# Rotary layer attention of an adaLN block: keys and queries normalised in place in PSUM, negated scores, another order of the norms

## Chip, core and metric

One core of a Trainium2 chip runs the whole block in one launch. The metric is device microseconds of that core, from the first to the last instruction of an execution. Engines are called as in the profile: PE (TensorE, PEld are its weight loads), DVE (VectorE), ACT (ScalarE), POOL (GpSimd), SP (SyncE).

## What is computed

The block takes 4 x 1024 tokens of width 256. A modulated layer norm is followed by a causal attention with 16 heads, then a second modulated norm is followed by two "layers", whose result is gated and added. The change touches only the local attention of those two layers (8 heads of 64, QK_SCALE 8, windows of 128 tokens that see themselves and the window before):

```python
def _layer(x, wqkv, qs, ksc, wo, lg, lb, w1, b1, w2, b2):
    h = shift_token(x)                       # second half of the channels from the token before
    q, k, v = split(h @ wqkv, 3)
    q = l2norm(q) * qs                       # per head of 64
    k = l2norm(k) * ksc
    q = q*cos*scale + rotate_half(q)*sin*scale
    k = k*cos/scale + rotate_half(k)*sin/scale
    sim = 8 * q k^T                          # own window and the one before
    sim = where(mask, -max, sim)
    x = x + (softmax(sim) @ v) @ wo
    ...                                      # shift, norm, gated gelu MLP, added to x
```

## The kernel before, in words

The work falls into phases: the first norm, the causal attention (about 1240 us), `phase_layers` (the rest but the last 30 us) and the output. `phase_layers` runs a loop over two layers. In each, the attention loops over 32 tiles of 128 tokens, two tiles to a turn of the hardware loop (`par` 0 and 1), and then an MLP loops over 8 chunks. Each engine has its instruction stream written out by hand, and semaphores order them. An engine takes its instructions strictly in the order written, so what stands behind a waiting instruction waits too.

The tiles are software-pipelined. In one turn for tile t:

- PE transposes probabilities of tile t (`probs_T`, L1407), multiplies them with the values (`values`, L1417), makes the scores (`scores`, L1397) of tile t and then t+1, projects tile t+2 (`project`, parts 2 for v, 0 for q, 1 for k; the lines are those of the helper, L74 to L76), transposes the rotated q and k of tile t+1 (`qk_T`, L1389), transposes the stream of tile t+3 (`stream_T`, L1367), the output (`out_T`, L1424) and projects it (`project_out`, L74 to L76).
- DVE rotates q and k of tile t+1 (`rotate`, L1171 and L1174), masks the scores and takes their maxima (`maxima`, L1203), makes the exponent's bias from maximum and inverse norm (L1206), the low halves of the split operands (L1195, L1152, L1153, L1221), the sums of squares of tile t+2 (`squared_norms`, L1160 and L1162) and the normalised output (`normalise_out`, L1212 and L1216), and adds to the stream (L1321).
- ACT takes the exponentials (`exps`, L1018), copies transposed probabilities out of PSUM (`copy_probs`, L1027), the high halves of q and k (`qk_hi`, L1006 and L1008), the squares (`squares`, L1001) and the high half of the output (`out_hi`, L1031).
- POOL raises the sums of squares to the power -0.5 (`inverse_norms`, L928 and L929), adds the two rotated parts (`add_rotated`, L933), stages a tile (L920) and carries one column from tile to tile (`carry_over`, L915 and L917).

The query's norm is not applied to q: it enters as the `scale` of the exponential, and in its bias. The key's norm is applied by one multiplication out of PSUM into the tile `ly_kn` in SBUF (L1186), from which the key is rotated.

The orders that matter below, of ACT and of DVE in the second half of a turn, and of PE there:

```python
# ACT
exps(l, t, g, 3, par); qk_hi(l, t + 1, 1 - par, 0); copy_probs(g, 3); qk_hi(l, t + 1, 1 - par, 1)
squares(l, t + 2, 0); squares(l, t + 2, 1); stream_hi(l, t + 3, 1 - par); out_hi(g)
# DVE
maxima(l, t, g, 3, par); qk_lo(..., 0); qk_lo(..., 1); normalise_out(g, par); stream_lo(l, t + 3, 1 - par)
maxima(l, t + 1, g + 1, 0, ...); out_lo(g); squared_norms(l, t + 2, 0); maxima(l, t + 1, g + 1, 1, ...)
squared_norms(l, t + 2, 1); x += ...
# PE
qk_T(l, t + 1, 0); qk_T(l, t + 1, 1); values(g, 2, v_slots); probs_T(g, 3); project(l, t + 2, par, 1)
values(g, 3, v_slots); stream_T(...); scores(l, t + 1, 0, ...); out_T(g); scores(l, t + 1, 1, ...); project_out(g)
```

Of the kernel before, what the change touches and what calls it, by code (L numbers as in the profile page):

```python
# [725 lines left out]
def phase_layers(nc, io, scr, keep):  # L726
# [5 lines left out]
    with ExitStack() as ctx:  # L732
# [18 lines left out]
        rq = a.sb("ly_rq", [P, 2, LH])  # L751
        rk = a.sb("ly_rk", [P, LH])
        kn = a.sb("ly_kn", [P, INNER])
# [5 lines left out]
        small = a.sb("ly_small", [P, 2, 2, 2])  # L759
# [6 lines left out]
        def cut(start, *shape):  # L766
# [3 lines left out]
            if len(shape) > 1:  # L770
# [41 lines left out]
                 "mx_done nb_done h_lo rc_done on_done red_done fl_done ra_done kn_done o_lo qkT_lo xa_done msk "  # L812
# [5 lines left out]
        DVE_SEMS = ("mx_done nb_done h_lo rc_done on_done red_done fl_done ra_done kn_done o_lo qkT_lo xa_done msk "  # L818
# [36 lines left out]
        with nc.Block() as block:  # L855
# [37 lines left out]
            def _(pool):  # L893
# [28 lines left out]
                def inverse_norms(l, t, par, extra=0):  # L922

                    n = nth_rotated(l, t)

                    hold(pool, s["tick"], (s["fl_done"], at(2 * nth_projected(l, t) + 2)), (s["kn_done"], at(n)),
                         (s["ex_done"], at(LP * (nth(l, t) - 1) + extra)))
                    pool.tensor_tensor(rk[:], norm2[:, 1, 1, :], expo[:], ALU.pow).then_inc(s["pw_done"], 1)  # L928
                    pool.tensor_tensor(rq[:, par, :], norm2[:, 0, 1, :], expo[:], ALU.pow).then_inc(s["pw_done"], 1)  # L929
# [10 lines left out]
                with pool.Fori(0, L) as l:  # L940
                    hold(pool, s["tick"], (s["ya_done"], at(NCH * l)))
                    stage_tile(0, 0)
                    stage_tile(1, 1)
                    carry_over(l, 0, 0, 0)
                    stage_tile(0, 2)
                    inverse_norms(l, 0, 0, LP)
                    add_rotated(l, 0, 0)
                    add_rotated(l, 0, 1)
                    carry_over(l, 1, 1, 1)
                    stage_tile(1, 3)  # L950
                    inverse_norms(l, 1, 1)
                    carry_over(l, 2, 0, 2)
                    with pool.Fori(0, B) as b, pool.Fori(0, TB // 2) as jj:
                        for par in range(2):
                            t = b * TB + jj * 2 + par
                            add_rotated(l, t + 1, 0)
                            add_rotated(l, t + 1, 1)
                            hold(pool, s["tick"], (s["xT_mm"], at(nth_transposed(l, t + 3))))
                            stage_tile(par, (t + 4) % NT)
                            carry_over(l, t + 3, 1 - par, (jj * 2 + par + 3) % TB)  # L960
                            inverse_norms(l, t + 2, par)
                    inverse_deviation(l, 0)
                    with pool.Fori(0, NCH) as c:
                        hold(pool, s["tick"], (s["xnd"], at(nth_norm(l, c) + 1)))
                        pool.tensor_tensor(x[:, ds(c * CT, CT), :], x[:, ds(c * CT, CT), :],
                                           b2[:].unsqueeze(1).broadcast_to([P, CT, D]), ALU.add).then_inc(s["b2_done"], 1)
                        inverse_deviation(l, c + 1)

            @block.scalar
            def _(act):  # L970
# [44 lines left out]
                def exps(l, t, g, j, par):  # L1015
                    hold(act, s["tick"], (s["nb_done"], at(nth_scores(l, t, j) + 1)))
                    for h in range(2):
                        step = act.activation(pr[:, j % 2, h, :], sm[:, j % 2, h, :], ACT.Exp,  # L1018
                                              bias=small[:, j % 2, 1, h:h + 1], scale=rq[:, par, 2 * j + h:2 * j + h + 1],
                                              accum_out=sums[:, par, 2 * j + h:2 * j + h + 1])  # L1020
                    step.then_inc(s["ex_done"], 1)
# [91 lines left out]
            def _(dve):  # L1113
# [63 lines left out]
                def rotate_q(l, t, w):  # L1177
                    rotate(l, t, 0, ps_qkv[0][:], w)

                def rotate_k(l, t, w):  # L1180
                    after(dve, "kn_done", nth_rotated(l, t) + 1)
                    rotate(l, t, 1, kn[:], w)

                def normalise_keys(l, t):
                    after(dve, "pw_done", 2 * nth_projected(l, t) + 1)
                    dve.tensor_tensor(kn[:].rearrange("p (h d) -> p h d", d=DH), ps_qkv[1][:].rearrange("p (h d) -> p h d", d=DH),  # L1186
                                      rk[:].unsqueeze(2).broadcast_to([P, LH, DH]), ALU.mult).then_inc(s["kn_done"], 1)
# [9 lines left out]
                def maxima(l, t, g, j, par):  # L1197

                    if j >= 2:
                        after(dve, "ex_done", LP * g + j - 1)  # L1200
                    hold(dve, s["tick"], (s["sc_mm"], at(nth_scores(l, t, j) + 1)))
                    for h in range(2):
                        dve.tensor_tensor_reduce(sm[:, j % 2, h, :], ps_s[h][:, 0:2 * P], mask[:, par].rearrange("p a b -> p (a b)"),  # L1203
                                                 1.0, -3.0e38, ALU.add, ALU.max, small[:, j % 2, 0, h:h + 1]).then_inc(s["mx_done"], 1)
                    after(dve, "mx_done", 2 * nth_scores(l, t, j) + 2)
                    dve.scalar_tensor_tensor(small[:, j % 2, 1, :], small[:, j % 2, 0, :], -1.0, rq[:, par, 2 * j:2 * j + 2],  # L1206
                                             ALU.mult, ALU.mult).then_inc(s["nb_done"], 1)
# [61 lines left out]
                with dve.Fori(0, L) as l:  # L1269
# [10 lines left out]
                    rotate_q(l, 0, 0)  # L1280
                    normalise_keys(l, 0)
                    rotate_k(l, 0, 0)
# [12 lines left out]
                    with dve.Fori(0, B) as b, dve.Fori(0, TB // 2) as jj:  # L1295
                        for par in range(2):
# [3 lines left out]
                            rotate_q(l, t + 1, w)  # L1300
                            maxima(l, t, g, 2, par)
                            normalise_keys(l, t + 1)
                            rotate_k(l, t + 1, w)
# [8 lines left out]
                            qk_lo(l, t + 1, 1 - par, 1)  # L1312
                            normalise_out(g, par)
# [3 lines left out]
                            squared_norms(l, t + 2, 0)  # L1317
                            maxima(l, t + 1, g + 1, 1, 1 - par)
                            squared_norms(l, t + 2, 1)
# [39 lines left out]
            def _(pe):  # L1359
# [10 lines left out]
                def project(l, t, par, i):  # L1370
# [6 lines left out]
                    if i == 1:  # L1377
                        after(pe, "kn_done", n)
# [82 lines left out]
                with pe.Fori(0, L) as l:  # L1461
# [17 lines left out]
                    with pe.Fori(0, B) as b, pe.Fori(0, TB // 2) as jj:  # L1479
                        for par in range(2):  # L1480
# [16 lines left out]
                            qk_T(l, t + 1, 1)  # L1497
                            values(g, 2, v_slots)
                            probs_T(g, 3)
                            project(l, t + 2, par, 1)  # L1500
# [10 lines left out]
                         (s["nb_done"], at((LP * NT + 2) * (l + 1))), (s["xa_done"], at(NT * (l + 1))))  # L1511
# [33 lines left out]
def rope_tables():  # L1545
# [11 lines left out]
    tables = np.stack([cos * scale, sin * scale, cos / scale, sin / scale]).astype(np.float32)  # L1557
# [3 lines left out]
def local_masks():  # L1561

    q, k = np.arange(P)[:, None], np.arange(P)[None, :]
    own = np.where(k <= q, 0.0, MASKED).astype(np.float32)
    before = np.where(k >= q, 0.0, MASKED).astype(np.float32)
    none = np.full((P, P), MASKED, np.float32)
# [56 lines left out]
```

## Time and profile before

| | before |
|---|---|
| device time, median of 3 runs | 2997.27 us |
| the three runs | 2996.97, 2997.27, 2999.57 us |
| profiled execution, first to last instruction | 2999.0 us |
| busy PE / DVE / ACT / POOL | 2509.8 / 2103.4 / 1630.0 / 864.7 us |
| PE, weight loads | 1960.9 us |
| mean granted TensorE clock, whole span | 0.949 |
| attention loops of the two layers, from their first tile | about 1303 to 1856 us and 2162 to 2713 us |

The page gives for the profiled execution its span; no longer time is listed for it, and the span lies within the range of the three runs. Busy time is a sum over phases with different limits. The two attention loops of the layers take about 1100 us of the span, and what a turn of them costs has to be read from its own timeline.

### The profile page before, as it was taken

The page shows a single profiled execution, that of the slowest core. Times are in us where ns is not written, and L with a number is a line of the kernel's source. Part 1 is how long each engine was busy: PE and PEld are TensorE (multiplying, and loading weights), DVE is VectorE, ACT ScalarE, POOL GpSimd, SP SyncE. Part 2 cuts the span into 40 slices and gives each one's busy share as a digit, 9 for nine tenths or more (in the row PEclk, how much of TensorE's full clock was granted, in tenths as well). Part 3 has the DMA queues.
Part 4 walks back from the last instruction along what each step waited for, and adds up shares of the span by engine and source line. Part 5 has one row for each costly group of instructions (what it writes and reads, how often), then busy time and mean ns, then how long its engine had stood idle before and what let it go on. Part 6 is the DMA issues. An engine that isn't in the chain of part 4 may idle for free. (4 is left out here: it accounts for less than half of the span.)

```text
span 2999.0 us, 68027 instructions
## 1 busy us (share of the span) xinstructions
PE 2509.8 (84%) x22296; PEld 1960.9 (65%) x22296; DVE 2103.4 (70%) x4501; ACT 1630.0 (54%) x3100; POOL 864.7 (29%) x732
## 2 busy tenths in 40 slices
PE   5699989989998998188998895799698989894996
PEld 3466656666666666177777774688577777773885
DVE  5588668858885885667777775566577777774656
ACT  2566556646664674356666664333466666662332
POOL 0233223313331332333333332111233333332111
PEclk7899999999999999599999998899899999997998
DMA  4400020010002000400000000100100000000003
GB/s 154 143 11 16 5 73 11 13 65 14 13 10 68 11 15 19 140 1 0 7 1 6 4 3 6 45 0 0 34 0 7 0 7 0 7 0 7 0 0 112
DMA packets 74546, 77.26 MB, mean 26 GB/s; under 512 B 4224, under 2 KB 67320, under 8 KB 72952
## 3 DMA queue, kind: packets, MB, share of 16 engines
q1 hardware_dynamic: 74488, 76.46, 7.8%
q8 instruction: 40, 0.66, 0.1%
q14 instruction: 18, 0.15, 0.0%
HBM read 55.48 MB, written 16.78 MB: 24 GB/s over the span
## 5 line engine op out<-in xcount | busy, mean ns | idle before, releaser
L501 ACT ACTIVATE at_p<-at_ps_s,at_shift 128x1024 f32<-128x1024 f32 (+3 forms) x384 | 343.0, 902 | 112.1 <-DVE at_p_lo L435 50.3
L74 PE MATMUL ly_ps<-ly_w_hi,ly_operands 128*128 128x256 f32 (+1 forms) x1048 | 372.6, 356 | 33.6 <-DVE ly_operands L1221 17.2
L435 DVE TENSOR_TENSOR at_p_lo<-at_p,at_p_hi 128x1024 f16<-128x1024 f32 (+3 forms) x384 | 391.4, 1019 | 12.1
L1018 ACT ACTIVATE ly_probs<-ly_masked,ly_small,ly_rq 128x256 f32<-128x256 f32 x512 | 303.5, 594 | 145.2 <-DVE ly_small L1206 145.0
L431 DVE CAST at_p_hi<-at_p 128x1024 f16<-128x1024 f32 (+3 forms) x384 | 283.0, 737 | 140.9 <-PE at_ps_o L569 100.9
L75 PE MATMUL ly_ps<-ly_w_lo,ly_operands 128*128 128x256 f32 (+1 forms) x1048 | 347.4, 332 | 0.0
L76 PE MATMUL ly_ps<-ly_w_hi,ly_operands 128*128 128x256 f32 (+1 forms) x1048 | 346.5, 331 | 0.0
L567 PE MATMUL at_ps_o<-at_v,at_p_hi 128*128 128x65 f16 x2304 | 249.5, 194 | 36.0 <-DVE at_p_lo L435 36.0
L567 PEld LDWEIGHTS at_ps_o<-at_v,at_p_hi 128*128 128x128 f16 x2304 | 209.6, 96 | 99.9 <-DVE at_p_lo L435 56.1
L1417 PEld LDWEIGHTS ly_ps<-ly_values,ly_probs_T 128*128 128x128 f32 x2048 | 258.5, 191 | 12.3 <-issue 0.8
L1417 PE MATMUL ly_ps<-ly_values,ly_probs_T 128*128 x2048 | 256.7, 268 | 0.0
L74 PEld LDWEIGHTS ly_ps<-ly_w_hi,ly_operands 128*128 128x128 f32 x1048 | 202.1, 193 | 73.3 <-issue 31.6
L568 PE MATMUL at_ps_o<-at_v,at_p_hi 128*128 128x64 f16 x2304 | 247.7, 194 | 0.0
L569 PE MATMUL at_ps_o<-at_v,at_p_lo 128*128 128x65 f16 x2304 | 246.1, 192 | 0.0
L74 PE MATMUL at_ps_m<-at_hT,at_w_hi 128*128 (+1 forms) x396 | 176.3, 445 | 65.0 <-DVE at_v L400 43.6
L1027 ACT ACTIVATE ly_probs_T<-ly_ps 128x512 f32<-128x512 f32 x256 | 150.4, 587 | 139.9 <-PE ly_ps L1417 121.7
L1203 DVE CUSTOM_DVE_ANT_0 ly_masked<-ly_ps,ly_mask 128x256 f32<-128x256 f32 x520 | 198.7, 419 | 24.7 <-DVE ly_mask L1308 11.7
L76 PEld LDWEIGHTS ly_ps<-ly_w_hi,ly_operands 128*128 128x128 f32 x1048 | 202.2, 193 | 19.1
L569 PEld LDWEIGHTS at_ps_o<-at_v,at_p_lo 128*128 128x128 f16 x2304 | 213.7, 99 | 0.0
L568 PEld LDWEIGHTS at_ps_o<-at_v,at_p_hi 128*128 128x128 f16 x2304 | 213.3, 97 | 0.4
L1195 DVE TENSOR_TENSOR ly_operands<-ly_ps,ly_operands 128x512 fp32r<-128x512 f32 x132 | 91.3, 692 | 173.0 <-ACT ly_operands L1006 128.6
L1397 PE MATMUL ly_ps<-ly_operands 64*128 64x256 f32 x1560 | 161.9, 313 | 60.6 <-DVE ly_small L1203 60.6
(208 smaller groups left out, 6331.1 us busy)
## 6 DMA issues: line engine op xcount, KB each, us to landing
at_hT<-hT_hi SPq DMA_DIRECT2D x5, 1024.0 KB, 5.0
at_hT<-hT_lo SPq DMA_DIRECT2D x5, 1024.0 KB, 8.1
at_w_raw<-in_Wv SPq DMA_DIRECT2D x34, 128.0 KB, 2.1
at_w_raw<-in_Wq SPq DMA_DIRECT2D x34, 128.0 KB, 2.3
at_w_raw<-in_Wk SPq DMA_DIRECT2D x34, 128.0 KB, 2.3
n_x<-in_states SPq DMA_DIRECT2D x4, 1024.0 KB, 11.6
hT_hi<-n_hi SPq DMA_DIRECT2D x8, 512.0 KB, 3.0
hT_lo<-n_lo SPq DMA_DIRECT2D x8, 512.0 KB, 3.1
```

What stands on the lines that cost most here:

```text
L74: pe.matmul(out, w_hi, x_hi, start=first, stop=False, skip_group_check=True)
L75: pe.matmul(out, w_hi, x_lo, start=False, stop=False, skip_group_check=True)
L76: return pe.matmul(out, w_lo, x_hi, start=False, stop=last, skip_group_check=True)
L431: dve.tensor_copy(p_hi[u % 2][:, :, off:], probs[u % 2][:, :, off:]).then_inc(p_hi_done, 1)
L435: dve.tensor_tensor(p_lo[u % 2][:, :, off:], probs[u % 2][:, :, off:], p_hi[u % 2][:, :, off:], ALU.subtract).then_inc(p_lo_done, 1)
L501: act.activation(probs[u % 2][:, :, off:], ps_s[u % 2][:, :, off:], ACT.Exp, bias=shift[:], scale=SCORE_SCALE).then_inc(exp_done, 1)
L567: pe.matmul(out, ph, ones_hi, start=(kt == 0 and t == 0), stop=False, skip_group_check=True)
L568: pe.matmul(out[:, 0:DH], ph, lo, start=False, stop=False, skip_group_check=True)
L569: step = pe.matmul(out, pl, ones_hi, start=False, stop=(kt == qc * CT + t), skip_group_check=True)
L1018: step = act.activation(pr[:, j % 2, h, :], sm[:, j % 2, h, :], ACT.Exp, bias=small[:, j % 2, 1, h:h + 1], scale=rq[:, par, 2 * j + h:2 * ...
L1203: dve.tensor_tensor_reduce(sm[:, j % 2, h, :], ps_s[h][:, 0:2 * P], mask[:, par].rearrange("p a b -> p (a b)"), 1.0, -3.0e38, ALU.add, ALU ...
L1417: step = pe.matmul(ps_pv[:, cols], pT[:, (2 * slot + h) * P:(2 * slot + h + 1) * P], vv[:, v_slots[slot], cols], start=(j == 0 and h == 0 ...
```

## The change

- q is no longer left unnormalised. POOL raises the norms of q and then of k into one tile `rn`; DVE multiplies q and k with them in place in PSUM and rotates both from PSUM (`normalise_and_rotate`). The SBUF tile `kn` is gone, and the exponential has the constant scale -1.
- The tables that rotate q are negated, so that the scores come out negated; the masks are positive, and the masked minimum is the bias of the exponential itself. The small DVE operation between maxima and exponential (L1206) and its semaphore are gone.
- DVE runs both `squared_norms` of tile t+2 right behind `qk_lo` and ahead of `normalise_out`.
- PE runs `project(t+2, 1)` ahead of `values(g, 2)` instead of behind `probs_T(g, 3)`, and it waits for all six rotations instead of for `kn`.
- POOL runs `inverse_norms(t+2)` ahead of `carry_over(t+3)`, and q's power waits only for q's sum.

Left out of the diff are the lists of semaphores, the calls ahead of the loop, which follow the same pattern, and PE's wait behind the loop, which takes `mx_done` for `nb_done`.

```diff
@@ -748,15 +748,13 @@
         expo = a.sb("ly_expo", [P, LH])
         sq = a.sb("ly_sq", [P, 2, INNER])
         norm2 = a.sb("ly_norm2", [P, 2, 2, LH])
-        rq = a.sb("ly_rq", [P, 2, LH])
-        rk = a.sb("ly_rk", [P, LH])
-        kn = a.sb("ly_kn", [P, INNER])
+        rn = a.sb("ly_rn", [P, 2, LH])
         xs = a.sb("ly_xs", [P, 2, D])
         ra = a.sb("ly_rope_a", [P, 2, INNER])
         rt = a.sb("ly_rope_t", [P, 2, INNER])
         sm = a.sb("ly_masked", [P, 2, 2, 2 * P])
         pr = a.sb("ly_probs", [P, 2, 2, 2 * P])
-        small = a.sb("ly_small", [P, 2, 2, 2])
+        nmax = a.sb("ly_nmax", [P, 2, 2])
         sums = a.sb("ly_sums", [P, 2, LH])
         rsum = a.sb("ly_rsum", [P, LH])
         vv = a.sb("ly_values", [P, V_RING, INNER])
...
@@ -919,14 +917,11 @@
                 def stage_tile(par, tile):
                     pool.tensor_copy(xs[:, par, :], x[:, tile, :]).then_inc(s["xs_done"], 1)
 
-                def inverse_norms(l, t, par, extra=0):
-
-                    n = nth_rotated(l, t)
-
-                    hold(pool, s["tick"], (s["fl_done"], at(2 * nth_projected(l, t) + 2)), (s["kn_done"], at(n)),
-                         (s["ex_done"], at(LP * (nth(l, t) - 1) + extra)))
-                    pool.tensor_tensor(rk[:], norm2[:, 1, 1, :], expo[:], ALU.pow).then_inc(s["pw_done"], 1)
-                    pool.tensor_tensor(rq[:, par, :], norm2[:, 0, 1, :], expo[:], ALU.pow).then_inc(s["pw_done"], 1)
+                def inverse_norms(l, t):
+
+                    for i, used in enumerate(("qn_done", "kn_done")):
+                        hold(pool, s["tick"], (s["fl_done"], at(2 * nth_projected(l, t) + i + 1)), (s[used], at(nth_rotated(l, t))))
+                        pool.tensor_tensor(rn[:, i, :], norm2[:, i, 1, :], expo[:], ALU.pow).then_inc(s["pw_done"], 1)
 
                 def add_rotated(l, t, i):
                     hold(pool, s["tick"], (s["ra_done"], at(6 * nth_rotated(l, t) + 3 * i + 3)))
...
@@ -957,8 +952,8 @@
                             add_rotated(l, t + 1, 1)
                             hold(pool, s["tick"], (s["xT_mm"], at(nth_transposed(l, t + 3))))
                             stage_tile(par, (t + 4) % NT)
+                            inverse_norms(l, t + 2)
                             carry_over(l, t + 3, 1 - par, (jj * 2 + par + 3) % TB)
-                            inverse_norms(l, t + 2, par)
                     inverse_deviation(l, 0)
                     with pool.Fori(0, NCH) as c:
                         hold(pool, s["tick"], (s["xnd"], at(nth_norm(l, c) + 1)))
...
@@ -1013,10 +1008,10 @@
                     act.activation(vv[:, slot, :], ps_qkv[2][:], ACT.Copy).then_inc(s["v_done"], 1)
 
                 def exps(l, t, g, j, par):
-                    hold(act, s["tick"], (s["nb_done"], at(nth_scores(l, t, j) + 1)))
+                    hold(act, s["tick"], (s["mx_done"], at(2 * nth_scores(l, t, j) + 2)))
                     for h in range(2):
                         step = act.activation(pr[:, j % 2, h, :], sm[:, j % 2, h, :], ACT.Exp,
-                                              bias=small[:, j % 2, 1, h:h + 1], scale=rq[:, par, 2 * j + h:2 * j + h + 1],
+                                              bias=nmax[:, j % 2, h:h + 1], scale=-1.0,
                                               accum_out=sums[:, par, 2 * j + h:2 * j + h + 1])
                     step.then_inc(s["ex_done"], 1)
 
...
@@ -1174,17 +1169,14 @@
                         dve.tensor_tensor(th[:, :, a0:a0 + half], zh[:, :, b0:b0 + half],
                                           sin[:, a0:a0 + half].unsqueeze(1).broadcast_to([P, LH, half]), ALU.mult).then_inc(s["ra_done"], 1)
 
-                def rotate_q(l, t, w):
-                    rotate(l, t, 0, ps_qkv[0][:], w)
-
-                def rotate_k(l, t, w):
-                    after(dve, "kn_done", nth_rotated(l, t) + 1)
-                    rotate(l, t, 1, kn[:], w)
-
-                def normalise_keys(l, t):
-                    after(dve, "pw_done", 2 * nth_projected(l, t) + 1)
-                    dve.tensor_tensor(kn[:].rearrange("p (h d) -> p h d", d=DH), ps_qkv[1][:].rearrange("p (h d) -> p h d", d=DH),
-                                      rk[:].unsqueeze(2).broadcast_to([P, LH, DH]), ALU.mult).then_inc(s["kn_done"], 1)
+                def normalise_and_rotate(l, t, i, w):
+
+                    done = ("qn_done", "kn_done")[i]
+                    after(dve, "pw_done", 2 * nth_projected(l, t) + i + 1)
+                    z = ps_qkv[i][:].rearrange("p (h d) -> p h d", d=DH)
+                    dve.tensor_tensor(z, z, rn[:, i, :].unsqueeze(2).broadcast_to([P, LH, DH]), ALU.mult).then_inc(s[done], 1)
+                    after(dve, done, nth_rotated(l, t) + 1)
+                    rotate(l, t, i, ps_qkv[i][:], w)
 
                 def qk_lo(l, t, par, i):
                     after(dve, "qkT_hi", 2 * nth_rotated(l, t) + i + 1)
...
@@ -1200,11 +1192,9 @@
                         after(dve, "ex_done", LP * g + j - 1)
                     hold(dve, s["tick"], (s["sc_mm"], at(nth_scores(l, t, j) + 1)))
                     for h in range(2):
-                        dve.tensor_tensor_reduce(sm[:, j % 2, h, :], ps_s[h][:, 0:2 * P], mask[:, par].rearrange("p a b -> p (a b)"),
-                                                 1.0, -3.0e38, ALU.add, ALU.max, small[:, j % 2, 0, h:h + 1]).then_inc(s["mx_done"], 1)
-                    after(dve, "mx_done", 2 * nth_scores(l, t, j) + 2)
-                    dve.scalar_tensor_tensor(small[:, j % 2, 1, :], small[:, j % 2, 0, :], -1.0, rq[:, par, 2 * j:2 * j + 2],
-                                             ALU.mult, ALU.mult).then_inc(s["nb_done"], 1)
+                        dve.tensor_tensor_reduce(sm[:, j % 2, h, :], ps_s[h][:, 0:2 * P],
+                                                 mask[:, par].rearrange("p a b -> p (a b)"),
+                                                 1.0, 3.0e38, ALU.add, ALU.min, nmax[:, j % 2, h:h + 1]).then_inc(s["mx_done"], 1)
 
                 def normalise_out(g, par):
                     after(dve, "ex_done", LP * g + LP)
...
@@ -1297,10 +1286,9 @@
                             t = b * TB + jj * 2 + par
                             g = nth(l, t)
                             w = (jj * 2 + par + 1) % TB
-                            rotate_q(l, t + 1, w)
+                            normalise_and_rotate(l, t + 1, 0, w)
                             maxima(l, t, g, 2, par)
-                            normalise_keys(l, t + 1)
-                            rotate_k(l, t + 1, w)
+                            normalise_and_rotate(l, t + 1, 1, w)
                             if par == 1:
 
                                 m = (NT // 2 + 1) * l + b * (TB // 2) + jj + 1
...
@@ -1310,13 +1298,13 @@
                             maxima(l, t, g, 3, par)
                             qk_lo(l, t + 1, 1 - par, 0)
                             qk_lo(l, t + 1, 1 - par, 1)
+                            squared_norms(l, t + 2, 0)
+                            squared_norms(l, t + 2, 1)
                             normalise_out(g, par)
                             stream_lo(l, t + 3, 1 - par)
                             maxima(l, t + 1, g + 1, 0, 1 - par)
                             out_lo(g)
-                            squared_norms(l, t + 2, 0)
                             maxima(l, t + 1, g + 1, 1, 1 - par)
-                            squared_norms(l, t + 2, 1)
                             after(dve, "wo_mm", g + 1)
                             dve.tensor_tensor(x[:, t, :], x[:, t, :], ps_misc[:, 0:D], ALU.add).then_inc(s["xa_done"], 1)
                     split_weights(4 * l + 2, F_COLS, 0)
...
@@ -1375,7 +1363,7 @@
                     if i == 0:
                         after(pe, "ra_done", 6 * n - 3)
                     if i == 1:
-                        after(pe, "kn_done", n)
+                        after(pe, "ra_done", 6 * n)
                     cols = slice(i * INNER, (i + 1) * INNER)
                     for k in range(KT):
                         step = three_products(pe, ps_qkv[i][:], hT[:, par, 0, k, 0:P], hT[:, par, 1, k, 0:P],
...
@@ -1495,9 +1483,9 @@
                             qk_T(l, t + 1, 0)
                             after(pe, "v_done", nth_projected(l, t + 2) + 1)
                             qk_T(l, t + 1, 1)
+                            project(l, t + 2, par, 1)
                             values(g, 2, v_slots)
                             probs_T(g, 3)
-                            project(l, t + 2, par, 1)
                             values(g, 3, v_slots)
                             after(pe, "qkT_lo", 2 * nth_rotated(l, t + 1) + 2)
                             stream_T(l, t + 3, 1 - par)
...
@@ -1554,16 +1542,16 @@
     scale = np.concatenate([scale, scale], axis=-1)
     sign = np.where(np.arange(DH) < DH // 2, -1.0, 1.0).astype(np.float32)
     cos, sin = np.cos(freqs), np.sin(freqs) * sign
-    tables = np.stack([cos * scale, sin * scale, cos / scale, sin / scale]).astype(np.float32)
+    tables = np.stack([-cos * scale, -sin * scale, cos / scale, sin / scale]).astype(np.float32)
     return np.ascontiguousarray(tables.reshape(4, TB, P, DH).transpose(2, 0, 1, 3).reshape(P, -1))
 
 
 def local_masks():
 
     q, k = np.arange(P)[:, None], np.arange(P)[None, :]
-    own = np.where(k <= q, 0.0, MASKED).astype(np.float32)
-    before = np.where(k >= q, 0.0, MASKED).astype(np.float32)
-    none = np.full((P, P), MASKED, np.float32)
+    own = np.where(k <= q, 0.0, -MASKED).astype(np.float32)
+    before = np.where(k >= q, 0.0, -MASKED).astype(np.float32)
+    none = np.full((P, P), -MASKED, np.float32)
 
     mask = np.stack([np.stack([own, before], axis=1), np.stack([before, own], axis=1)], axis=1)
     return {"mask": mask, "prev_mask": np.stack([none] + [before] * (TB // 2 - 1), axis=1)}
...
```

## Rows read from the trace of the kernel before

**Rows 1.** Timeline of ACT, L1031, once a tile: start us, us, engine, line, what.

```profile
1299.23 0.60 ACT L1031 ACTIVATE ly_operands<-ly_ps 128x512 fp32r<-128x512 f32 x1 [0.62 <-PE ly_ps L1424]
...
1844.92 0.60 ACT L1031 ACTIVATE ly_operands<-ly_ps 128x512 fp32r<-128x512 f32 x1 [0.62 <-PE ly_ps L1424]
```

**Rows 2.** Waits of PE, 1303 to 1856 us: in total, times, longest.

```profile
PE ly_ps L1397 <- DVE ly_small L1203: 26.8, 31, 1.1
PE ly_ps L1389 <- POOL ly_rope_a L933: 19.7, 30, 0.9
```

**Rows 3.** Timeline of PE, one tile, 1619 to 1638 us.

```profile
1619.66 0.60 PE L1407 MATMUL ly_ps<-ident,ly_probs 128*128 128x128 f32 x4
...
1626.89 0.60 PE L1389 MATMUL ly_ps<-ident,ly_rope_a 128*128 128x128 f32 x4
1628.01 0.66 PE L1389 MATMUL ly_ps<-ident,ly_rope_a 128*128 128x128 f32 x4 [0.52 <-POOL ly_rope_a L933]
1628.50 1.00 PE L1417 MATMUL ly_ps<-ly_values,ly_probs_T 128*128 x8
1629.43 0.66 PE L1407 MATMUL ly_ps<-ident,ly_probs 128*128 128x128 f32 x4
1629.84 0.48 PE L74 MATMUL ly_ps<-ly_w_hi,ly_operands 128*128 128x512 f32 x1
...
1631.32 1.00 PE L1417 MATMUL ly_ps<-ly_values,ly_probs_T 128*128 x8
...
1637.07 0.60 PE L1407 MATMUL ly_ps<-ident,ly_probs 128*128 128x128 f32 x4
```

**Rows 4.** Timeline of ACT in the same tile.

```profile
1630.12 0.60 ACT L1027 ACTIVATE ly_probs_T<-ly_ps 128x512 f32<-128x512 f32 x1 [0.27 <-PE ly_ps L1407]
1630.62 0.59 ACT L1008 ACTIVATE ly_operands<-ly_ps 128x512 fp32r<-128x512 f32 x1
1631.10 1.18 ACT L1001 ACTIVATE ly_sq<-ly_ps 128x512 f32<-128x512 f32 x2
```

**Rows 5.** Timeline of DVE in the same tile.

```profile
1623.22 0.68 DVE L1186 TENSOR_TENSOR ly_kn<-ly_ps,ly_rk 128x512 f32<-128x512 f32 x1
1624.05 0.69 DVE L1171 TENSOR_TENSOR ly_rope_a<-ly_kn,ly_rope 128x512 f32<-128x512 f32 x1
...
1631.85 0.19 DVE L1212 RECIPROCAL ly_rsum<-ly_sums 128x8 f32<-128x8 f32 x1
1632.42 0.69 DVE L1216 TENSOR_TENSOR ly_on<-ly_ps,ly_rsum 128x512 f32<-128x512 f32 x1 [0.38 <-DVE ly_rsum L1212]
...
1635.35 0.67 DVE L1160 TENSOR_REDUCE ly_norm<-ly_sq 128x8 f32<-128x512 f32 x1
...
1636.32 0.42 DVE L1203 CUSTOM_DVE_ANT_0 ly_masked<-ly_ps,ly_mask 128x256 f32<-128x256 f32 x1
...
1637.30 0.69 DVE L1160 TENSOR_REDUCE ly_norm<-ly_sq 128x8 f32<-128x512 f32 x1
...
1638.15 0.42 DVE L1321 TENSOR_TENSOR stream<-stream,ly_ps 128x256 f32 x1
```

**Rows 6.** Durations by line: min/median/max ns; the second is of the page's part 5.

```profile
L1171 DVE TENSOR_TENSOR ly_rope_a<-ly_kn,ly_rope x66: 691/693/1839, 1262.9 to 2698.8; 128x512 f32<-128x512 f32 x66
...
L933 POOL TENSOR_TENSOR ly_rope_a<-ly_rope_a,ly_rope_t 128x512 f32<-128x512 f32 x132 | 175.8, 1332 | 75.8 <-DVE ly_rope_t L1174 75.8
```

**Rows 7.** Stretches: us, busy PE, PEld, DVE, ACT, POOL, PE clock, DMA share, GB/s.

```profile
1315.11:1318.52 3.41, 2.02 (x19) 1.38 (x18) 2.86 (x10) 1.76 (x6) 0.19 (x1) 1.00 0.02 5
1318.53:1321.94 3.41, 3.41 (x16) 3.16 (x16) 2.73 (x10) 1.83 (x6) 0.51 (x1) 0.50 0.02 5
1632.55:1635.96 3.41, 2.27 (x21) 1.66 (x20) 3.06 (x10) 2.05 (x6) 0.19 (x1) 1.00 0.00 0
```

**Rows 8.** Timeline of ACT, L1031, around the second of these stretches.

```profile
1316.61 0.60 ACT L1031 ACTIVATE ly_operands<-ly_ps 128x512 fp32r<-128x512 f32 x1 [0.62 <-PE ly_ps L1424]
1335.39 0.60 ACT L1031 ACTIVATE ly_operands<-ly_ps 128x512 fp32r<-128x512 f32 x1 [0.63 <-PE ly_ps L1424]
```

More of the change, by code:

```diff
@@ L811, in phase_layers @@
                  "h_hi ex_done sq_done pt_done o_hi qkT_hi v_done "
-                 "mx_done nb_done h_lo rc_done on_done red_done fl_done ra_done kn_done o_lo qkT_lo xa_done msk "
+                 "mx_done h_lo rc_done on_done red_done fl_done ra_done qn_done kn_done o_lo qkT_lo xa_done msk "
                  "ca_in ca_out pw_done add_done xs_done "
@@ L817, in phase_layers @@
         ACT_SEMS = "h_hi ex_done sq_done pt_done o_hi qkT_hi v_done w_hi_done warmed ff_done f_hi gl_done"
-        DVE_SEMS = ("mx_done nb_done h_lo rc_done on_done red_done fl_done ra_done kn_done o_lo qkT_lo xa_done msk "
+        DVE_SEMS = ("mx_done h_lo rc_done on_done red_done fl_done ra_done qn_done kn_done o_lo qkT_lo xa_done msk "
                     "w_lo_done rope_q bn ag vr nr xnd f_lo uf_done u_lo ya_done")
@@ L945, in _ @@
                     stage_tile(0, 2)
-                    inverse_norms(l, 0, 0, LP)
+                    inverse_norms(l, 0)
                     add_rotated(l, 0, 0)
@@ L950, in _ @@
                     stage_tile(1, 3)
-                    inverse_norms(l, 1, 1)
+                    inverse_norms(l, 1)
                     carry_over(l, 2, 0, 2)
@@ L1279, in _ @@
                     squared_norms(l, 0, 1)
-                    rotate_q(l, 0, 0)
-                    normalise_keys(l, 0)
-                    rotate_k(l, 0, 0)
+                    normalise_and_rotate(l, 0, 0, 0)
+                    normalise_and_rotate(l, 0, 1, 0)
                     qk_lo(l, 0, 0, 0)
@@ L1510, in _ @@
                     hold(pe, s["tick"], (s["sq_done"], at(2 * (NT + 2) * (l + 1))),
-                         (s["nb_done"], at((LP * NT + 2) * (l + 1))), (s["xa_done"], at(NT * (l + 1))))
+                         (s["mx_done"], at(2 * (LP * NT + 2) * (l + 1))), (s["xa_done"], at(NT * (l + 1))))
                     chunk_T(l, 0)
```

## The prediction

> **What bounds the kernel now.** I read the stretches of the trace first, to find where the changed code runs: two attention loops of 32 tiles each. ACT's copy of the output stands once in each tile, so its first and last start in one loop give the period: (1844.92 - 1299.23) / 31 = 17.60 us [rows 1]. The reader should see there that 64 tiles are 1126 us, and that a microsecond per tile is 64 us of the kernel.
>
> Then the waits of PE. Over one loop they are 26.8 us on the masked scores and 19.7 us on the rotated keys [rows 2], together 46.5 / 31 = 1.5 us per tile. PE works in the other 16: it is nearly the bound, so whatever is to be won here is small, and what makes PE wait longer is paid in full.
>
> Last the timelines of one tile, from one start of the first probability transposition to the next, 1619.66 to 1637.07, 17.41 us [rows 3]. Read backwards from the next tile: project_out waits for the output's low half, that for ACT's copy, that for out_T, and out_T for the normalised output `ly_on` on DVE (1632.42). This DVE operation waits now for the last `values` on PE (begun 1631.32, lasting 1.00) and not for DVE: the reciprocal before it had long begun (1631.85) [rows 3, 5]. So the loop's chain is: PE up to the last values, DVE `ly_on`, then 1637.07 - 1632.42 = 4.65 us of out_T, copy, low half and project_out, then PE again.
>
> **The change part by part.**
>
> *PE's order.* I count from the start of the tile's first transposition. The first qk_T starts at 7.23 and takes about 0.49 (as from the second, 1628.01, to values, 1628.50); the second starts at 8.35, so it waited 8.35 - 7.72 = 0.63 us for the keys [rows 3]. After the change that wait goes (next part). But project(1), 1631.32 - 1629.84 = 1.48 us, now stands ahead of values(2), 0.93 us (1628.50 to 1629.43). The last probs_T starts at 7.72 + 0.49 + 1.48 + 0.93 = 10.62 instead of 9.77. Project(1) was the cover for ACT's copy of these probabilities: the copy starts 0.69 us after probs_T and lasts 0.60 [rows 3, 4], so without cover the last values starts 1.35 us after probs_T instead of 1.89 (0.06 for the handover). That is 11.97, against 11.66: PE alone loses only 0.3 us here, and idles 0.9 us that it had worked.
>
> *The norms ahead of the output.* This is the expensive edit. On ACT the order is unchanged: copy of the probabilities, high half of the keys, the two squares. The copy waits for the last probs_T, so all of them hang on it: high half of the keys 1.19 us, squares 1.67 us after probs_T, and both squares done at 2.85 [rows 3, 4]. DVE takes the low half of the keys and is ready for the reciprocal 1631.85 - 1629.43 = 2.42 us after probs_T [rows 3, 5]. Now two squared norms stand there. One costs DVE 1636.32 - 1635.35 = 0.97 or 1638.15 - 1637.30 = 0.85 us, to the start of what follows [rows 5]; the mean is 0.91, two are 1.82. The squares come in time for them. The reciprocal then starts at 4.24 after probs_T. From it to `ly_on` there are 0.57 us now, in part the wait for PE; without that the reciprocal's own 0.19 and a handover remain, so from 0.27 to 0.57, and I take the middle, 0.42. `ly_on` starts at 4.66 after probs_T instead of 2.99. Behind it wait, on DVE, the low half of the stream and maxima(0) of the next tile; PE has done its scores by then and waits for `ly_on`.
>
> *Sum per tile with the clock as it is.* 10.62 + 4.66 + 4.65 = 19.93 us, against 17.60: 2.33 us more, bounds 2.2 to 2.5 from the handover.
>
> *Normalising in place, and the rotations.* DVE gains an operation per tile, q times its norm. For a write into PSUM no row exists; the nearest is the same multiplication out of PSUM into SBUF, 0.68 us [rows 5]. Below, it could be somewhat faster than that; above, I take twice, 1.4 us. With the wait for itself it fills 1624.05 - 1623.22 = 0.83 us [rows 5]. It loses the small operations between maxima and exponential, four per tile, and rotates the keys from PSUM: from `ly_kn` the first product took 691 ns at best and 1839 at worst, while POOL added [rows 6]. None of this counts in the sum: DVE has the stream's addition behind it about 0.8 us into PE's next tile, then q 0.83 and its rotation 1.26 (as in this timeline), maxima 0.70 (two of 0.35), k 0.83 + 1.26, that is keys rotated at 5.7. POOL adds them in 1.33 [rows 6] and 0.26 of handover, at 7.3, and PE asks for them at 7.72. So there is 0.4 us of room. If the product in PSUM costs double (twice 0.69 us), 1.4 - 0.4 = 1.0 us per tile comes on top. The removed small operation also brings ACT the exponentials earlier, but the last of these is needed at 10.62 and comes at about 9.3.
>
> *POOL's order.* The two powers start right behind q's sum, while DVE is busy with norms and output; q's is needed in the next tile. The carried column is now written behind two powers, and next read by project(2) of the next tile, over 2 us later. Nothing is added. The first tiles of each layer have a little more and a little less in chain, within 2 us for both layers; I take 0.
>
> *The clock.* From the last probs_T on, PE would be busy 0.66, idle 0.7, busy 1.0, idle 0.2, busy 1.0, idle 1.7, busy 0.65 (out_T), idle 0.5, busy 0.6, idle 0.7. The 3.4 us around the largest gap hold about 1.3 us of work. Now, of two stretches of 3.41 us at the same place in a tile, one with 2.27 us of PE work was followed by full clock, one with 2.02 by a stretch of 3.41 us at 0.50, that is 1.2 for 2.4 GHz [rows 7]. The fall at 1318.5 lengthened its tile to 1335.39 - 1316.61 = 18.78 us, 1.2 us over the mean [rows 1, 8]. I expect a fall in nearly every tile. In the new order part of the slow stretch lies over PE's own waits, where it is cheap (about 0.5 us), part over dense projections (3.41 us at half speed do 1.95 us of such work, 1.5 us lost). I take 1.0 per tile, the middle, 64 us in all, bounds 0 and 1.5.
>
> The Trainium skill ("TensorE: Matmul & The Clock Gate", Part 1 with "HAM oscillation") gives as its abstract rule that gaps without any matmul, of a length that no gap of this loop reaches, bring the slow clock. By this rule there would be no fall here, and the time would be that of the first rival. The trace speaks against it: no gap before the fall at 1318.5 was over 1.1 us, PE's longest wait in the loop [rows 2].
>
> **Sum.** 64 x 2.33 = 149 and 64 x 1.0 = 64, together 213 us, on the profiled execution's 2999 us: 3212 us. That execution's span is 2 us above the median of the runs shown, which is 2997; I give 3210.
>
> **The rivals.**
>
> *The clock holds.* For: PE's longest new gap is 1.7 us. Against: the row with 2.02 us of work. It gives 2997 + 149 = 3146 us.
>
> *The write into PSUM is dear.* At double cost the keys come 1.0 us late in every tile, and the order above still holds: 3210 + 64 = 3274 us. For: no DVE operation of this loop writes PSUM, so nothing excludes it. Against: the reads from PSUM cost no more than from SBUF (0.68 us out of PSUM, 0.69 out of SBUF) [rows 5].
>
> *Faster.* If DVE is what the loop hangs on, its lighter stretch (no `ly_kn` slowed by POOL, no small operations) is passed on, and the norms and projections find room in waits. At best all waits of rows 2 go, 1.5 x 64 = 96 us; with the keys' wait alone, 19.7 / 31 x 64 = 41 us, so 2956 us. It decides if `ly_on` does not start later than 3.0 us after a last probs_T that is itself no later than 9.8. For: the keys' wait is real. Against: two norms in series on DVE directly before `ly_on`.
>
> *No change.* The gain of the keys and of the maxima would have to meet the loss of the norms exactly; I see nothing for it.
>
> **How the numbers follow.** Forecast (falls in most tiles) 0.62; clock holds 0.23; dear write 0.07; faster 0.04; the rest, about nothing, 0.02 and a still longer slow clock 0.02. A difference below 0.2%, 6 us, can't be told from none. So slower 0.93, same 0.03, faster 0.04. The range reaches from the clock that holds with the lower handover, 2997 + 64 x 2.2 = 3138, less a little for terms rounded up, 3125, to falls at 1.4 us each, 2997 + 149 + 90 = 3236, and a part of a dear write: 3260.
>
> **What would show it right or wrong.** The distance of two L1031 starts should be near 20.9 us (19.9 if the clock holds). On PE, out_T (L1424) should wait for `ly_on` by over 1.5 us per tile, the last values for the copy by about 0.8, and qk_T no longer for POOL. On DVE, two L1160 should stand between L1195 and L1212. The clock of the loops should be near 0.9 instead of 0.99. It would be wrong if the reciprocal starts less than 3 us after the last probs_T, if PE waits at qk_T for the keys still, or if the period is below 17.6.

## The result, and the profile after

The changed kernel takes 3258.7 us (median of 4 runs, 3255.4 to 3261.7), against 2998.4 us (2997.0 to 3000.3) of the kernel before on the same chip: a ratio of 1.086, 95% interval 1.085 to 1.088. The forecast was 3210 us, range 3125 to 3260. The direction and the mechanism were right, and the time lies at the upper end of the range: one term, the slow clock, was sized too small, and the longer chain somewhat too large.

The period comes from ACT's copy of the output (now L1026), first and last of the first loop, which answers to [rows 1]:

```profile
1298.68 0.60 ACT L1026 ACTIVATE ly_operands<-ly_ps 128x512 fp32r<-128x512 f32 x1 [2.08 <-PE ly_ps L1412]
...
1970.53 0.60 ACT L1026 ACTIVATE ly_operands<-ly_ps 128x512 fp32r<-128x512 f32 x1 [2.55 <-PE ly_ps L1412]
```

(1970.53 - 1298.68) / 31 = 21.67 us, against 17.60. The second loop has 21.64. 64 x 4.07 = 260 us is the whole difference, so it lies in the two loops of 32 tiles. The waits of PE from 1300 to 1840 us (in total, times, longest) answer to [rows 2]:

```profile
PE ly_ps L1412 <- DVE ly_on L1206: 33.9, 25, 1.4
PE ly_ps L1405 <- ACT ly_probs_T L1022: 19.3, 25, 0.8
PE ly_ps L74 <- DVE ly_operands L1211: 16.8, 25, 0.7
PE ly_ps L1355 <- DVE ly_operands L1187: 6.5, 25, 0.3
```

The waits of before, for the masked scores and for the keys, are gone. In their place PE waits, 25 times in 25 tiles, at out_T for the normalised output, at the last values for the copied probabilities, and at project_out. The next two fences are the timelines of PE and then of DVE in one tile; they answer to [rows 3] and [rows 5].

```profile
1618.71 0.61 PE L1395 MATMUL ly_ps<-ident,ly_probs 128*128 128x128 f32 x4
1620.09 1.10 PE L1405 MATMUL ly_ps<-ly_values,ly_probs_T 128*128 x8 [0.77 <-ACT ly_probs_T L1022]
1621.45 0.44 PE L1355 MATMUL ly_ps<-ident,ly_xs 128*128 128x128 f32 x2 [0.26 <-DVE ly_operands L1187]
1621.82 0.63 PE L1385 MATMUL ly_ps<-ly_operands 64*128 64x256 f32 x6
1623.85 1.11 PE L1412 MATMUL ly_ps<-ident,ly_on 128*128 128x128 f32 x4 [1.41 <-DVE ly_on L1206]
...
1626.63 0.55 PE L74 MATMUL ly_ps<-ly_w_hi,ly_operands 128*128 128x256 f32 x1 [0.69 <-DVE ly_operands L1211]
...
1629.33 0.71 PE L1395 MATMUL ly_ps<-ident,ly_probs 128*128 128x128 f32 x4
```

```profile
1621.08 0.68 DVE L1155 TENSOR_REDUCE ly_norm<-ly_sq 128x8 f32<-128x512 f32 x1
...
1621.96 0.69 DVE L1155 TENSOR_REDUCE ly_norm<-ly_sq 128x8 f32<-128x512 f32 x1
...
1622.87 0.20 DVE L1202 RECIPROCAL ly_rsum<-ly_sums 128x8 f32<-128x8 f32 x1
1623.10 0.69 DVE L1206 TENSOR_TENSOR ly_on<-ly_ps,ly_rsum 128x512 f32<-128x512 f32 x1
```

The reader should see the series: the two sums (1621.08, 1621.96), then the reciprocal 4.16 us after the last probs_T (1618.71), `ly_on` 4.39 us after it (before: 2.99), and only then out_T. A second thing shows in the durations: out_T takes 1.11 us. In the kernel before it was

```profile
1633.17 0.66 PE L1424 MATMUL ly_ps<-ident,ly_on 128*128 128x128 f32 x4
```

The clock is low there. Two stretches of the same tile (us, busy PE, PEld, DVE, ACT, POOL, then PE clock), which answer to [rows 7]:

```profile
1615.60:1622.40 6.80, 5.76 (x44) 4.79 (x43) 2.59 (x5) 4.35 (x12) 0.17 (x1) 1.00 0.00 0
1622.80:1629.40 6.60, 4.86 (x23) 4.23 (x24) 3.40 (x14) 2.79 (x9) 2.94 (x4) 0.50 0.00 0
```

For 6.6 us and a little more the clock stands at 0.50, 1.2 GHz. Before it fell, PE had waited 0.77 and 0.26 us, and it was waiting for `ly_on`. It is back at full only with the next tile's first transpositions. In this loop the clock fell once in each of the 31 tiles; 10 of these stretches lasted about 10 us, the others about 6.8.

### The profile page after: what moved, and what is told of

It reads as the page before. It is cut to its first block and busy times, and to the rows that moved or that the text cites. A ratio compares the mean times of both kernels' runs of the same rounds, so it can differ in the third digit from the quotient of the medians.

```text
span 3257.1 us, 67705 instructions
## 1 busy us (share of the span) xinstructions
PE 2684.5 (82%) x22296; PEld 2103.9 (65%) x22296; DVE 2024.0 (62%) x4307; ACT 1569.9 (48%) x3100; POOL 851.0 (26%) x732
## 5 line engine op out<-in xcount | busy, mean ns | idle before, releaser
L74 PE MATMUL ly_ps<-ly_w_hi,ly_operands 128*128 128x256 f32 (+1 forms) x1048 | 415.0, 396 | 60.3 <-DVE ly_operands L1211 43.7
L75 PE MATMUL ly_ps<-ly_w_lo,ly_operands 128*128 128x256 f32 (+1 forms) x1048 | 384.0, 366 | 0.0
L76 PE MATMUL ly_ps<-ly_w_hi,ly_operands 128*128 128x256 f32 (+1 forms) x1048 | 380.0, 363 | 0.0
L924 POOL TENSOR_TENSOR ly_rn<-ly_norm,ly_expo 128x8 f32<-128x8 f32 x136 | 221.2, 1643 | 462.4 <-DVE ly_norm L1157 462.4
L928 POOL TENSOR_TENSOR ly_rope_a<-ly_rope_a,ly_rope_t 128x512 f32<-128x512 f32 x132 | 168.9, 1279 | 536.3 <-DVE ly_rope_t L1169 536.3
L74 PEld LDWEIGHTS ly_ps<-ly_w_hi,ly_operands 128*128 128x128 f32 x1048 | 237.4, 227 | 108.5 <-issue 68.9
L1405 PE MATMUL ly_ps<-ly_values,ly_probs_T 128*128 x2048 | 263.4, 272 | 49.5 <-ACT ly_probs_T L1022 49.5
L1013 ACT ACTIVATE ly_probs<-ly_masked,ly_nmax 128x256 f32<-128x256 f32 x512 | 254.6, 500 | 42.3 <-DVE ly_nmax L1195 36.6
L567 PEld LDWEIGHTS at_ps_o<-at_v,at_p_hi 128*128 128x128 f16 x2304 | 209.3, 96 | 100.4 <-DVE at_p_lo L435 56.7
L76 PEld LDWEIGHTS ly_ps<-ly_w_hi,ly_operands 128*128 128x128 f32 x1048 | 239.7, 229 | 20.0
L75 PEld LDWEIGHTS ly_ps<-ly_w_lo,ly_operands 128*128 128x128 f32 x1048 | 241.3, 230 | 11.9
```

Of the source, the lines that this page charges most:

```text
L74: pe.matmul(out, w_hi, x_hi, start=first, stop=False, skip_group_check=True)
L75: pe.matmul(out, w_hi, x_lo, start=False, stop=False, skip_group_check=True)
L76: return pe.matmul(out, w_lo, x_hi, start=False, stop=last, skip_group_check=True)
L567: pe.matmul(out, ph, ones_hi, start=(kt == 0 and t == 0), stop=False, skip_group_check=True)
L924: pool.tensor_tensor(rn[:, i, :], norm2[:, i, 1, :], expo[:], ALU.pow).then_inc(s["pw_done"], 1)
L1405: step = pe.matmul(ps_pv[:, cols], pT[:, (2 * slot + h) * P:(2 * slot + h + 1) * P], vv[:, v_slots[slot], cols], start=(j == 0 and h == 0 ...
```

## The experiments

All times are medians of four runs; the kernel before stood at 2998.3 to 2998.6 us beside them. The time per tile and the clock are those of the first loop, from its first to its last copy of the output.

| kernel | us | ratio, 95% interval | us per tile | clock in the loop |
|---|---|---|---|---|
| before | 2998.4 | | 17.60 | 1.00 |
| changed | 3258.7 | 1.085 to 1.088 | 21.67 | 0.81 |
| e1, norms back | 3118.8 | 1.039 to 1.043 | 19.36 | 0.90 |
| e2, project(1) back | 3175.4 | 1.058 to 1.061 | 20.41 | 0.84 |
| e3, all orders back | 2957.3 | 0.985 to 0.988 | 16.95 | 1.00 |
| e4, changed + 11 matmuls a tile | 3182.9 | 1.060 to 1.063 | 20.50 | 0.94 |
| e5, changed + 15 matmuls a tile | 3121.8 | 1.039 to 1.043 | 19.54 | 1.00 |
| e6, before with keys in PSUM | 2961.3 | 0.986 to 0.989 | 17.03 | 1.00 |
| e7, e3 with keys in SBUF | 2959.3 | 0.986 to 0.989 | 16.95 | 1.00 |
| e8, before with norms ahead | 3131.4 | 1.042 to 1.046 | 19.71 | 0.91 |
| e9, e1 + 3 matmuls a tile | 3039.7 | 1.012 to 1.015 | 18.32 | 0.98 |

**e1, the norms back.** The squared norms and POOL's powers go to their old places in the changed kernel (POOL's lines are not shown).

```diff
-    squared_norms(l, t + 2, 0)
-    squared_norms(l, t + 2, 1)
     normalise_out(g, par)
     ...
     out_lo(g)
+    squared_norms(l, t + 2, 0)
     maxima(l, t + 1, g + 1, 1, 1 - par)
+    squared_norms(l, t + 2, 1)
```

> The changed kernel with both squared norms back in their old places behind out_lo and behind maxima(1), and POOL's powers back behind the carried column; project(1) stays early, the normalisation in PSUM stays. My theory (norms in series ahead of the output, plus slow clock): the output's normalisation starts 3.0 us after the last probs_T again, so a tile is 10.62 + 2.99 + 4.65 = 18.3 us and the clock holds: 2998 + 64 x 0.66 = 3040 us. Rival (the normalisation in PSUM and the longer work of DVE are what costs): stays near 3250 us.

It took 3119 us instead of 3040. Taking the norms back is worth 140 us, less than I expected: the clock fell here too (0.90). The mean is 19.36 us per tile; the three tiles of 17.90 us are the shortest, the sum had 18.3.

**e2, project(1) back.**

```diff
-    project(l, t + 2, par, 1)
     values(g, 2, v_slots)
     probs_T(g, 3)
+    project(l, t + 2, par, 1)
     values(g, 3, v_slots)
```

> The changed kernel with PE's project(1) back behind the last probs_T, the norms ahead of the output as changed. My theory: the last probs_T starts at about 9.4 instead of 10.6 us of the tile and the norms still cost their 1.8 us: a tile of 18.4 us with full clock, up to 20 with slow stretches, 3050 to 3150 us. Rival (PE's order is the cause): back to 3000 us or below.

It took 3175 us, above my range of 3050 to 3150: 20.41 us per tile, beyond even the 20 that I gave for slow stretches, with the clock at 0.84. The rival, PE's order as the only cause, falls.

**e3, all orders back.** Both edits of e1 and e2. What is left of the change is the normalisation in PSUM, the negated scores and the maximum as bias.

> The changed kernel with the orders of the kernel before on DVE, PE and POOL: only the normalisation in PSUM, the negated scores and the maximum as bias are left of the change. My theory: these save; the wait of PE for the keys shrinks and the last probs_T starts at about 9.4 us, a tile of 17.0 us, 2955 us (2940 to 2985). Rival (the write in PSUM and q's extra operation on DVE cost): 3050 to 3250 us. Second rival (nothing on the chain is touched): 2995 to 3000 us.

2957.3 us, faster than the kernel before by 41 us and than the changed one by 301. So these parts save, and the two orders cost more than the whole difference. They overlap: put back first, the norms give 140 and project(1) 83 us; put back last, 218 and 161. The row of PE's waits, first loop, 1300 to 1840 us:

```profile
PE ly_ps L1385 <- DVE ly_nmax L1195: 25.6, 31, 0.8
PE ly_ps L74 <- DVE ly_operands L1211: 6.7, 31, 0.2
```

The wait for the keys [rows 2] is not there any more; that for the masked scores nearly stayed as it was (26.7 us in these 540 us of the kernel before).

**e4 and e5, work in the waits.** If the clock falls because PE waits, then matmuls that nobody needs, put into the waits, must bring it up and make the kernel faster. They write a PSUM bank that is free at that place. This is e5's edit; where e4 differs is marked.

```diff
+def filler(n, bank=ps_pt):
+    for i in range(n):
+        pe.matmul(bank[:], w_hi[:, 0:P], w_hi[:, 0:CH], start=True, stop=True, skip_group_check=True)
...
     probs_T(g, 3)
+    filler(3, ps_s[0])        # e5 alone
     values(g, 3, v_slots)
     ...
     scores(l, t + 1, 0, 1 - par)
+    filler(7)                 # e4: 6
     out_T(g)
+    filler(2)
     scores(l, t + 1, 1, 1 - par)
+    filler(3)
     project_out(g)
```

> The changed kernel with 11 more matmuls per tile on PE (6 ahead of out_T, 2 ahead of scores(1), 3 ahead of project_out, 128x128 by 512 columns, about 0.22 us each at full clock), written into the bank of transposed probabilities after it was read; they lie in PE's waits and change no other engine. If the slow clock costs the difference between 19.9 us and the 21.6 us per tile measured, the clock of the loops is near 1.0 and the time falls to 3130 to 3170 us although PE does more. If the clock is not the cause, the time stays at 3258 us or rises by up to 64 x 1 us.

> As the kernel with 11 more matmuls per tile, with 3 further ones in the wait of PE between the last probs_T and the last values (into a bank of scores that is free there) and 7 instead of 6 ahead of out_T. In the kernel with 11, tiles in which the clock held took 19.3 and 19.7 us and the mean was 20.5. If the clock is what remains, it holds in nearly all tiles now: mean 19.5 us per tile, 2998 + 64 x 1.9 = 3120 us (3110 to 3150). If the added work itself delays, the time is at or above 3183 us.

3183 and 3122 us; the first is above its range of 3130 to 3170, the second inside its own. Filling the waits wins 76 us; filling the one ahead of the last values as well wins 61 more. In e5 the first loop reads:

```profile
1300.00:1840.00 540.00, 530.12 (x3625) 434.10 (x3624) 338.28 (x1008) 279.24 (x778) 176.76 (x195) 1.00 0.01 3
```

With 15 needless matmuls per tile, the kernel is 137 us faster than without. That separates the two costs, though only to a bound, since the added matmuls delay PE a little themselves: PE no longer waits for `ly_on` at all in e5, and out_T starts 0.99 us after `ly_on` instead of 0.75.

```profile
1610.99 0.69 DVE L1206 TENSOR_TENSOR ly_on<-ly_ps,ly_rsum 128x512 f32<-128x512 f32 x1
```

```profile
1611.98 0.60 PE L1416 MATMUL ly_ps<-ident,ly_on 128*128 128x128 f32 x4
```

At full clock the change costs at most 19.54 - 17.60 = 1.94 us per tile, 124 us, and the slow clock at least 21.67 - 19.54 = 2.13 us per tile, 136 us. The 1.94 us are the orders less what the rest of the change saves (e3). In e4 a tile in which the clock held (1.00 from 1386.57 to 1405.89) took 19.32 us, with out_T 0.75 us behind `ly_on`; by it an estimate is 1.7 us for the change at full clock and 2.35 for the clock.

e4 shows one thing more. The waits at out_T and at project_out, which lie in the changed kernel's slow time, are filled, and in 22 of its 23 falls the slow stretch is about 3.4 us long, against 6.8 to 10. So the waits inside the slow time are what prolonged it.

**e9, the same for e1.** The three matmuls ahead of the last values, put into e1.

> As the changed kernel with norms and powers in their old places and project(1) early (measured 3119 us, 19.36 us per tile, 17.90 in the tiles in which the clock held), with 3 more matmuls per tile in the 0.77 us that PE waits there between the last probs_T and the last values. Theory (the early project(1) costs little by itself and the rest is slow clock that this uncovered wait brings): 17.9 to 18.0 us per tile with the clock near 1.0, 2998 + 64 x 0.35 = 3020 us (3010 to 3050). Rival (the early projection itself costs 1.8 us per tile): 3119 us or more.

3039.7 us and 18.32 us per tile (the expectation was 17.9 to 18.0), with the clock at 0.98. e9 is e3 with the early project(1) and the filling, e1 the same without filling. So the early project(1) costs 3039.7 - 2957.3 = 82 us by itself (a rest of slow clock in it), and through the clock 3118.8 - 3039.7 = 79 us more, though the longest wait of PE in e1 is 0.9 us.

**e8, the norms alone, in the kernel before.**

```diff
+    squared_norms(l, t + 2, 0)
+    squared_norms(l, t + 2, 1)
     normalise_out(g, par)
     ...
     out_lo(g)
-    squared_norms(l, t + 2, 0)
     maxima(l, t + 1, g + 1, 1, 1 - par)
-    squared_norms(l, t + 2, 1)
```

> The kernel before with both squared norms ahead of the output's normalisation and nothing else changed. Theory (norms in series ahead of the output, then slow clock): out_T waits over 1 us for the normalised output, a tile of 18.4 us with full clock, near 19.8 with slow stretches, 3120 to 3180 us. Rival (the norms only cost together with the early projection or the normalised q): below 3020 us.

3131 us, 19.71 per tile. Tiles in which the clock held took 18.4 us, as expected. The rival, norms that cost only together with the other edits, falls. DVE's timeline shows the same series without any other edit of the change:

```profile
1612.79 0.68 DVE L1160 TENSOR_REDUCE ly_norm<-ly_sq 128x8 f32<-128x512 f32 x1
...
1613.67 0.69 DVE L1160 TENSOR_REDUCE ly_norm<-ly_sq 128x8 f32<-128x512 f32 x1
...
1614.58 0.20 DVE L1212 RECIPROCAL ly_rsum<-ly_sums 128x8 f32<-128x8 f32 x1
1614.81 0.69 DVE L1216 TENSOR_TENSOR ly_on<-ly_ps,ly_rsum 128x512 f32<-128x512 f32 x1
```

**e6, where the saving comes from.** The kernel before, with the key's multiplication in place in PSUM.

```diff
-dve.tensor_tensor(kn[:]..., ps_qkv[1][:]..., rk..., ALU.mult)
+dve.tensor_tensor(ps_qkv[1][:]..., ps_qkv[1][:]..., rk..., ALU.mult)
-rotate(l, t, 1, kn[:], w)
+rotate(l, t, 1, ps_qkv[1][:], w)
-after(pe, "kn_done", n)
+after(pe, "ra_done", 6 * n)
```

> The kernel before with one thing changed: the keys are multiplied by their norm in place in PSUM and rotated from there, project(1) waits for the rotations. Theory (the 41 us that the change saves with the old orders are the two-SBUF-input products of the key rotation, which POOL holds up by 1.0 us per tile): PE's wait for the keys goes, 2955 to 2975 us. Rival (the saving is the small operation between maxima and exponential, and the exponential with constant scale): 2990 to 3000 us.

2961.3 us: this one edit gives 37 of the 41 us, and its interval overlaps that of e3. The rival, the small operation and the exponential's scale, falls.

**e7, the keys in SBUF again,** with everything else as in e3. PE's project(1) waits for `kn_done` again; that line and the tile's allocation are not shown.

```diff
 z = ps_qkv[i][:]
-dve.tensor_tensor(z, z, rn[:, i, :]..., ALU.mult)
+dst = (ps_qkv[0][:], kn[:])[i]
+dve.tensor_tensor(dst, z, rn[:, i, :]..., ALU.mult)
-rotate(l, t, i, ps_qkv[i][:], w)
+rotate(l, t, i, dst, w)
```

> The changed kernel with all the old orders, and the normalised keys written to an SBUF tile and rotated from there again; q stays in PSUM, scores negated. Theory (the key products slowed by POOL): the gain is lost again, 2990 to 3015 us, with products of up to 1.8 us on DVE. Rival (small operation and exponential): 2957 to 2970 us.

2959.3 us: my expectation of 2990 to 3015 failed, nothing is lost. All 31 key products out of SBUF in e7's first loop took 0.69 us. The kernel before, POOL and then DVE:

```profile
1606.63 1.29 POOL L933 TENSOR_TENSOR ly_rope_a<-ly_rope_a,ly_rope_t 128x512 f32<-128x512 f32 x1
```

```profile
1606.65 1.82 DVE L1171 TENSOR_TENSOR ly_rope_a<-ly_kn,ly_rope 128x512 f32<-128x512 f32 x1
```

and e7, POOL and then DVE:

```profile
1608.80 1.29 POOL L929 TENSOR_TENSOR ly_rope_a<-ly_rope_a,ly_rope_t 128x512 f32<-128x512 f32 x1 [0.88 <-DVE ly_rope_t L1170]
1611.59 1.27 POOL L929 TENSOR_TENSOR ly_rope_a<-ly_rope_a,ly_rope_t 128x512 f32<-128x512 f32 x1 [1.50 <-DVE ly_rope_t L1170]
```

```profile
1610.05 0.69 DVE L1167 TENSOR_TENSOR ly_rope_a<-ly_kn,ly_rope 128x512 f32<-128x512 f32 x1
```

Before, POOL's addition of the query began 0.02 us ahead of the key's product, which took 1.82 instead of 0.69 us. That is so in every second tile of the first loop. In the others, as in that of [rows 5], the first product takes 0.69 us and the next two, into the other rotated part, meet the addition (1624.38 on POOL, 1624.66 on DVE) and take 1.84 us instead of 0.75:

```profile
1624.38 1.50 POOL L933 TENSOR_TENSOR ly_rope_a<-ly_rope_a,ly_rope_t 128x512 f32<-128x512 f32 x1
```

```profile
1624.66 1.84 DVE L1174 TENSOR_TENSOR ly_rope_t<-ly_kn,ly_rope 128x256 f32<-128x256 f32 x2
```

So the keys lose about 1.1 us in every tile. In e7 the multiplication of q with its norm has moved the key's product back and the powers no longer hold up POOL's addition: it ends at 1610.09, and the product begins at 1610.05. The two hardly meet. In e6 they do meet (POOL's addition at 1627.47, the product at 1627.49), and the product, now out of PSUM, takes 0.69 us all the same. So two different edits each take away one and the same collision, and once PE no longer waits for the keys there is nothing more to win there. I read this from the start times; no run moved one of the two operations by itself.

## Why the prediction came out as it did

- *PE's order.* Forecast: the last probs_T at 10.62 us of the tile. In the tile from 1607.78 it starts at 10.93, with that tile's first 1.3 us at the slow clock; in e5, at full clock, at 10.34 (median). So this term was 0.28 us too large. The copy's lost cover: the last values 1.38 us after probs_T, forecast 1.35. Right.
- *The norms ahead of the output.* Reciprocal 4.16 us after probs_T (forecast 4.24), `ly_on` 4.39 (forecast 4.66: from reciprocal to `ly_on` it is 0.23 us, where 0.42 was taken and 0.27 was the lower bound). The series is right, and e8 shows it alone. The sign that out_T would wait over 1.5 us for `ly_on` missed by a little: the longest wait is 1.4.
- *Sum at full clock.* Forecast 2.33 us per tile, by e5 at most 1.94. In e5 the three terms are 10.34, 4.39 and 4.76 (medians), against 10.62, 4.66 and 4.65. The sum also set a tile of the shorter kind against the mean: for the tile of [rows 3] the same three terms give 9.77 + 2.99 + 4.65 = 17.41, not 17.60. Like against like it would have forecast 2.52, so the slip of 0.19 hid part of the excess.
- *Normalising in place.* Taken as 0.68 us as into SBUF; measured 0.69 (median 694 ns of 132). Right. The rival of a dear write falls, and PE waits for the keys no more.
- *The clock.* This is the term of the sum that was mis-sized: forecast 1.0 us per tile, bounds 0 and 1.5, measured at least 2.13. I had expected one fall of 3.41 us per tile, as in the only example in the loop of before [rows 7], where PE was fully busy right after it. A fall came in every tile, but the slow time was 6.8 to 10 us long: in the tile shown most of the wait at out_T (about 1.1 us) and 0.69 us at project_out lie in it, and in e4, with both filled, it is 3.4 us. The idle 0.5 us that the forecast had behind out_T did not come: scores(1) starts there without a wait (1624.93). The loop's clock was 0.81, where I had said near 0.9.
- *The rival of a clock that holds*, at 3146 us: refuted. The Trainium skill ("TensorE: Matmul & The Clock Gate", "HAM oscillation") gives the rule by which only long gaps bring the slow clock. These traces do not agree with it: no wait of PE in e1's loop is over 0.9 us, and its clock is 0.90.
- *The rival "faster".* Its condition failed, since `ly_on` starts 4.39 us after the last probs_T. Its price for the keys' wait alone, 2956 us, is what e3 (2957) and e6 (2961) measured once the orders were taken out.

The two errors were of opposite sign, -0.39 and +1.13 us per tile as e5 divides them. Together 64 x 0.74 = 47 us, they are nearly the whole distance of 49 us from 3210 to the measured time. That the time fell inside the range owes something to luck: the clock's term lay outside its own bounds, and the chain's excess made up for a third of what it lacked.

The version to keep is e3, 1.4% faster than the kernel before, or e6 where the smallest edit is wanted.

## What to carry to other kernels

Before an independent operation is put ahead of one that another engine waits for, count what starts only when that one is done; here 1.8 us of norms, not needed before the next tile, stood before the whole output chain. An instruction that covers another engine's latency (here a projection behind a transposition) is lost as a cover when it is moved up, even where it waits for nothing there. And where the trace shows a clock that falls after waits, price a new wait by a kernel in which the wait is filled, and check in its trace how far the filling delays the engine itself: here at least 136 us of the 260 came through the clock, and at most 124 from the longer chain.

## What had not been expected of the hardware

- Matmuls that do nothing useful made the kernel faster: 3258.7 to 3121.8 us, with the loop's clock from 0.81 to 1.00.
- With constant scale the exponential (128x256, accumulated) takes 497 ns in e3 (median of 512), with a scale per partition from SBUF 590 in the kernel before. e3 and e6 hardly differ (2957.3 and 2961.3 us), so neither this nor the small operation ahead of it was worth much on the chain.
